# The weight and context loads of a fused attention and feed-forward kernel divided between two DMA queues by partition half

## The reference, cut to what matters

```python
def bit_quant(w):                                 # ternary weights
    scale = jnp.maximum(jnp.mean(jnp.abs(w)), 1e-8)
    return jnp.clip(jnp.round(w / scale), -1.0, 1.0)   # value in the forward pass
...
query = ctx @ Wq.T + bq            # per batch: 512 x 128
key   = ctx @ Wk.T + bk
attention = softmax(query @ key.T, axis=-1)         # 512 x 512
x = x + layernorm(x) @ attention.T
h = gelu(layernorm(x) @ bit_quant(w1).T + b1)       # w1: 2048 x 512
x = x + h @ bit_quant(w2).T + b2                    # w2: 512 x 2048
```

## Time and profile before

| | |
|---|---|
| median of 3 runs | 321.32 us (320.93 to 323.28) |
| the profiled execution | 320.93 us |
| its span in the profile | 319.1 us |
| TensorE busy | 304.6 us (95%) |
| VectorE, ScalarE, GpSimd busy | 166.8, 144.0, 117.4 us |
| DMA moved | 28.04 MB, mean 88 GB/s |
| granted TensorE clock | 1.0 throughout |

### The profile page before, as it was taken

The page is one execution under the profiler, slowest core; times in us unless marked ns, Lnnn a source line. Parts: engine busy times, 40 slices in busy tenths (PEclk is TensorE's granted clock), DMA queues, the critical chain, the costliest instruction groups (busy, mean ns, idle before and its releaser), DMA issues.

```text
span 319.1 us, 3686 instructions
## 1 busy us (share of the span) xinstructions
PE 304.6 (95%) x1397; PEld 143.7 (45%) x1397; DVE 166.8 (52%) x295; ACT 144.0 (45%) x251; POOL 117.4 (37%) x129
## 2 busy tenths in 40 slices
PE   7999979969987999999999999999999999999995
PEld 3465534434433444444444444444444444444455
DVE  2788868898689881754425630553424103342101
ACT  2287776686450652455374332456350006772000
POOL 0385369938998993000460560000470000000000
PEclk9999999999999999999999999999999999999999
DMA  8999999992100499000003947000016110000011
GB/s 198 271 209 211 213 137 219 214 278 68 31 0 0 87 175 267 0 2 0 0 0 69 174 89 199 0 0 0 2 31 130 39 66 0 0 2 0 33 62 40
DMA packets 57922, 28.04 MB, mean 88 GB/s; under 512 B 42800, under 2 KB 51760, under 8 KB 57904
## 3 DMA queue, kind: packets, MB, share of 16 engines
q1 hardware_dynamic: 57536, 27.53, 40.9%
q10 hardware_dynamic: 368, 0.27, 0.3%
HBM read 15.21 MB, written 4.19 MB: 61 GB/s over the span
## 4 chain that ended last, share of the span: by engine, by line
PE 73%; DMA 8%; SPq 8%; DVE 6%; ACT 3%; issue 2%
PE ps_e L526 31%; PE ps_t L509 29%; DMA w_raw<-in_L_ffn_w 7%; PE ps_e L494 6%; SPq L260 6%; PE ps_e L435 2%; PE ps_e L533 2%; PE ps_e L443 2%; ACT abs_out L695 1%; DVE tern L886 1%; DMA ctx_sb<-in_ctx 1%; SPq L277 1%; SPq L252 1%; DVE gT_lo L899 1%; DVE ctxT L763 1%
## 5 line engine op out<-in xcount | busy, mean ns | idle before, releaser
L509 PE MATMUL ps_t<-x2T,w1T 128*128 128x512 f16 x512 | 112.5, 379 | 0.0
L526 PE MATMUL ps_e<-w_raw,gT_hi 128*128 128x512 f16 x240 | 91.1, 380 | 3.0 <-DVE w_raw L893 3.0
L526 PE MATMUL ps_e<-w_raw,gT_lo 128*128 128x512 f16 x240 | 91.1, 380 | 0.0
L703 ACT ACTIVATE ps_t<-ps_t,b_col 128x512 f32<-128x512 f32 x64 | 42.2, 663 | 94.4 <-PE ps_t L509 94.4
L899 DVE SCALAR_TENSOR_TENSOR gT_lo<-ps_t,h_scale,gT_hi 128x512 f16<-128x512 f32 x64 | 44.9, 743 | 64.6 <-ACT gT_hi L708 64.6
L509 PEld LDWEIGHTS ps_t<-x2T,w1T 128*128 128x128 f16 x512 | 50.1, 98 | 60.6 <-issue 0.7
L905 DVE SCALAR_TENSOR_TENSOR x_sb<-ps_e,h_unscale,x_sb 128x512 f32<-128x512 f32 x15 | 11.2, 747 | 57.5 <-PE ps_e L526 57.5
L708 ACT ACTIVATE gT_hi<-ps_t,h_scale 128x512 f16<-128x512 f32 x64 | 40.3, 685 | 0.0
L526 PEld LDWEIGHTS ps_e<-w_raw,gT_hi 128*128 128x128 f16 x240 | 23.4, 98 | 33.1 <-DVE w_raw L893 4.5
L526 PEld LDWEIGHTS ps_e<-w_raw,gT_lo 128*128 128x128 f16 x240 | 23.5, 98 | 29.0 <-issue 1.7
L363 POOL TENSOR_SCALAR var_eps<-mv 128x4 f32<-128x4 f32 (+1 forms) x5 | 1.0, 196 | 81.4 <-DVE mv L835 81.4
(11 more groups left out here) (90 smaller groups left out, 276.6 us busy)
## 6 DMA issues: line engine op xcount, KB each, us to landing
w_raw<-in_L_ffn_w SPq DMA_DIRECT2D x16, 512.0 KB, 10.0
x_sb<-in_x SPq DMA_DIRECT2D x4, 1024.0 KB, 8.2
out<-x_sb SPq DMA_DIRECT2D x15, 256.0 KB, 2.5
ctx_sb<-in_ctx SPq DMA_DIRECT2D x16, 128.0 KB, 3.4
b_sb<-in_L_ffn_b SPq DMA_DIRECT2D x1, 256.0 KB, 8.6
out<-x_sb SPq DMA_DIRECT2D x2, 128.0 KB, 2.3
x2n<-in_L_xattn_Wq ACTq DMA_DIRECT2D x1, 128.0 KB, 2.9
x2n<-in_L_xattn_Wk ACTq DMA_DIRECT2D x1, 128.0 KB, 3.8
```

What stands on the lines that cost most here:

```text
L509: mm = nc.tensor.matmul(ps_t[t][:], w1T[:, k // 2, j, :, k % 2], x2T[:, b % 2, v, :, j], start=(v == 0 and j == 0), stop=(v == 1 and j == ...
L526: mm = nc.tensor.matmul(y_bank(t)[:], part[:, k, t * P:(t + 1) * P], w2T[:, k], start=(k == 0 and part is gT_hi), stop=(k == NF - 1 and pa ...
L703: nc.scalar.activation(ps_t[t][:], ps_t[t][:], ACT.Gelu, scale=1.0 / LN_SCALE, bias=b1_col[:, k:k + 1]).then_inc(gelu_done, 1)
```

## The change

Loads of the partition quarters 0 and 1 (EVEN) of both weights and of ctx 0 and 1 stay on SyncE's queue; those of quarters 2 and 3 (ODD) are issued by ScalarE, between its computations. The second half of `w2` and ctx 2 are now issued before the transposes of `x2`. ScalarE sums all eight chunks of `w2` as well, all before the first `gelus`; VectorE's `abs_sums` goes. `total(W2)` on TensorE comes before `hidden(0, 1)`. On VectorE, `turn_ctx(2)`, `abs_rows(W2)` and `quantiser_scale(W2)` come earlier.

```diff
+        EVEN, ODD = (0, 1), (2, 3)
+
+        def start_ctx(engine, b, quarters):
+            for q in quarters:
+                engine.dma_start(ctx_sb[q * R:(q + 1) * R], ctx_view[b, q]).then_inc(ctx_here, 16)
+
+        def start_w(engine, m, h, quarters):
+            n = raws[m].shape[1] // 2
+            for q in quarters:
+                engine.dma_start(raws[m][q * R:(q + 1) * R, h * n:(h + 1) * n, :],
+                                 w_views[m][q, :, h * n:(h + 1) * n, :]).then_inc(w_here[m][h], 16)
...
-            load_ctx(0)
+            start_ctx(sp, 0, EVEN)
             load_x(0)
...
-            load_ctx(1)
+            sp.wait_ge(ctxT_ready, 1)
+            start_ctx(sp, 1, EVEN)
             load_x(1)
-            load_w(0, 0)
-            load_w(0, 1)
-            load_w(1, 0)
+            start_w(sp, 0, 0, EVEN)
+            start_w(sp, 0, 1, EVEN)
+            start_w(sp, 1, 0, EVEN)
+            start_w(sp, 1, 1, EVEN)
+            sp.wait_ge(ctxT_ready, 2)
+            start_ctx(sp, 2, EVEN + ODD)
             turn_first_x2(0)
             turn_first_x2(1)
-            load_w(1, 1)
-            load_ctx(2)
...
             hidden(0, 0)
-            hidden(0, 1)
             pe.wait_ge(x2_done, 2 * NT)
             total(W2, ps_e[3])
+            hidden(0, 1)
             hidden(0, 2)
...
+            start_ctx(act, 0, ODD)
             act.dma_start(W_raw[:, 0, :], Wq).then_inc(W_here, 16)
             act.dma_start(W_raw[:, 1, :], Wk).then_inc(W_here, 16)
...
+            act.wait_ge(ctxT_ready, 1)
+            start_ctx(act, 1, ODD)
             act.wait_ge(bqk_here, 16 * 2)
             copy_qk(0)
+            start_w(act, 0, 0, ODD)
             exps(0)
+            start_w(act, 0, 1, ODD)
             copy_qk(1)
             high_turned_xn(0)
             high_turned_probs(0)
+            start_w(act, 1, 0, ODD)
+            sum_abs(0, [0])
             exps(1)
             high_turned_xn(1)
-            sum_abs(0, range(4))
+            start_w(act, 1, 1, ODD)
+            sum_abs(0, (1, 2, 3))
             high_turned_probs(1)
-            sum_abs(0, (4, 5))
-            high_x2(0, (0, 1))
-            sum_abs(0, (6, 7))
-            high_x2(0, (2, 3))
-            sum_abs(1, range(4))
+            sum_abs(0, (4, 5, 6, 7))
+            high_x2(0)
+            sum_abs(1, range(NCH))
             act.wait_ge(h_scale_done, 1)
             gelus(0, 0)
-            sum_abs(1, range(4, NCH - ABS_BY_DVE))
             gelus(0, 1)
...
             aggregate2(0, (2, 3))
-            low_x2(0, (0, 1))
             abs_rows(W1)
             residual(1, 0)
             quantiser_scale(W1)
-            low_x2(0, (2, 3))
+            low_x2(0)
+            turn_ctx(2)
             residual(1, 1)
...
             quantise(0, 3)
+            abs_rows(W2)
             low_gelus(0, (0, 1))
             quantise(0, 4)
             low_gelus(0, (2, 3))
-            abs_sums()
+            quantiser_scale(W2)
             quantise(0, 5)
             low_gelus(0, (4, 5))
-            abs_rows(W2)
+            quantise(0, 6)
             low_gelus(0, (6, 7))
-            quantise(0, 6)
-            quantiser_scale(W2)
             quantise(0, 7)
             low_gelus(0, (8, 9))
-            turn_ctx(2)
             quantise(1, 0)
```

More of the change, by code:

```diff
@@ L175, in xattn_ffn @@
         zeros_done, minus_half_done, ones_done = sem("zeros_done"), sem("minus_half_done"), sem("ones_done")
-        xn0_read, abs_by_dve = sem("xn0_read"), sem("abs_by_dve")
+        xn0_read = sem("xn0_read")
         ctxT_ready, b1_col_done, b1_abs_done = sem("ctxT_ready"), sem("b1_col_done"), sem("b1_abs_done")
@@ L193, in n_hidden @@
             return 3 + GROUPS * b + g
-        ABS_BY_DVE = 2
         def xn_bank(b, j):
@@ L247, in _ @@
         def _(sp):
-            def load_ctx(b):
-                if b:
-                    sp.wait_ge(ctxT_ready, b)
-                for q in range(Q):
-                    sp.dma_start(ctx_sb[q * R:(q + 1) * R], ctx_view[b, q]).then_inc(ctx_here, 16)
             def load_x(b):
                 sp.dma_start(x_sb[:, b], x_tiles[b]).then_inc(x_here[b], 16)
-            def load_w(m, h):
-                n = raws[m].shape[1] // 2
-                for q in range(Q):
-                    sp.dma_start(raws[m][q * R:(q + 1) * R, h * n:(h + 1) * n, :],
-                                 w_views[m][q, :, h * n:(h + 1) * n, :]).then_inc(w_here[m][h], 16)
             def turn(dst, stage, v, here):
@@ L314, in _ @@
             load_x(3)
-            load_ctx(3)
+            sp.wait_ge(ctxT_ready, 3)
+            start_ctx(sp, 3, EVEN + ODD)
             turn_x2(1)
@@ L835, in aggregate2 @@
                     nc.vector.bn_aggr(mv2[:, t], stats2[:, t]).then_inc(mv2_done, 1)
-            def abs_sums():
-                flat = w2_raw[:].rearrange("p a b -> p (a b)")
-                dve.wait_ge(w_here[1][1], 16 * Q)
-                for c in range(NCH - ABS_BY_DVE, NCH):
-                    nc.vector.tensor_reduce(abs_sum[:, 1, c:c + 1], flat[:, c * CH:(c + 1) * CH], AX.X, ALU.add,
-                                            apply_absolute_value=True).then_inc(abs_by_dve, 1)
             def abs_rows(m):
-                dve.wait_ge(abs_done, NCH if m == W1 else 2 * NCH - ABS_BY_DVE)
-                if m == W2:
-                    dve.wait_ge(abs_by_dve, ABS_BY_DVE)
+                dve.wait_ge(abs_done, NCH * m)
                 nc.vector.tensor_reduce(abs_row[:, m:m + 1], abs_sum[:, m - 1], AX.X, ALU.add).then_inc(abs_row_done, 1)
```

## The result

The changed kernel takes 330.47 us (median of 4 runs, 329.69 to 332.56) beside 321.12 us of the kernel before on the same chip: ratio 1.029, 95% interval 1.023 to 1.035. The forecast was 317.9 us, the range 316.0 to 327.0. The sign is wrong and the time lies above the range. The span of the profiled execution is 328.8 us against 319.1, +9.7.

The account below looks back on a forecast made before the run. TensorE, busy 95% of the span, was taken as the bound, so only its gaps could be won: -2.3 - 0.5 - 0.4 = -3.2 us gave 317.7, and half of the median's 0.4 on top 317.9 us; range 316.0 to 327.0.

Parts of the forecast that it names:

- The start, +0.4 us: At project(0): Wk behind two more ScalarE issues, start at 8.2 instead of 7.78 us; +0.4, bounds 0 and +0.8.
- ScalarE's issues, 1.5 us in bounds of 0 to 3: In ScalarE's queue: the fourth quarter of w1, issued behind exps(0), may block 0 to 3 us; 1.5 taken.
- The slack there is 0.97 us: On ScalarE before the second copy_qk(1) at 19.40: 0.97 us of slack to take up a blocked issue.
- Rival 4: ScalarE's issues block over 3 us or are slower; each us beyond moves hidden(0, 1) by one: 319 to 321, chance 0.15.
- The load rate, the disputed cost: Weight loads: even and odd quarters flow beside each other, 300 GB/s for w1 and 350 for w2, from 210 and 214.
- `w2` landed by 45: Sign to look for in the weight loads: w2 landed by 45 us instead of 63.64, with no wait of ScalarE.
- Nothing in the rows shows HBM or the DMA engines full: Argument for the higher weight load rates: no row shows HBM or DMA engines full at 210 GB/s.
- rival 3: Weight loads run at a rate of 240 to 280 GB/s: 319 to 324 us, chance 0.12.
- rival 2: Halves don't flow together, 210 to 225 GB/s; late ctx 2 blocks VectorE at turn_ctx(2): 326 to 330 us, chance 0.21.
- Where the gain remains: From hidden(0, 2) on: -2.3 there, -0.5 from turn_ctx(2) done early, -0.4 in output(0, 0).
- 2.6 us missing in `output(0, 0)`: Sign to look for in output(0, 0): of 3.0 us of gaps only 0.4 goes, about 2.6 us still missing.
- the sum: Whole kernel: -2.3 - 0.5 - 0.4 = -3.2 us against the profiled execution, the start inside hidden(0, 1)'s +0.5.

Follow-up runs that it names:

- e5: a with x 0 held back until ctx 0, Wq and Wk have landed, and x 1 until ctx 1 has: 323.31 us, ratio 1.008.
- e3: b with only the odd quarters of ctx 0 and 1 issued by ScalarE, weights, sums and order as before: 327.37 us, ratio 1.019.
- e11: e2 with the x2 order of b and the odd quarters of w1's second half issued behind high_turned_probs(0): 329.9 us, ratio 1.023.
- the loads alone: A separate kernel of loads only, in eleven stages, computing nothing, run once: w1 211 GB/s on one queue, 275 divided; w2 218 and 330.
- e2: a with ctx 0 and 1 wholly back on SyncE's queue, so only the weights are divided: median 324.01 us, ratio 0.999.
- e10: e2 with the order of b for high_x2, low_x2 and the sums: median 322.85 us, ratio 1.001.
- e7: b with only the two odd quarters of w2's second half issued by ScalarE, behind high_x2(0, (2, 3)): 326.02 us, ratio 1.018.
- e14: e10 with odd weight quarters issued by GpSimd: two behind x 0, two behind normalise_probs(0), four behind layernorm(1): 325.51 us, ratio 1.011.
- e8: e2 with ScalarE's later weight issues moved behind exps(1), high_turned_xn(1) and high_turned_probs(1): 327.44 us, ratio 1.017.
- e4: a with every load on SyncE's queue, in the changed order: 330.34 us, ratio 1.027.
- a: The changed kernel, against the kernel before: 330.47 us, ratio 1.029.
- e9: a with 21 warm-up products on TensorE instead of 10: 333.36 us, ratio 1.037.
- b: The kernel before the change: 321.12 us on the chip where the changed kernel was measured.

## Why the prediction was wrong

**The step that failed** is "The start, +0.4 us", with its bounds of 0 and +0.8 and "TensorE has next to no gap from there to 42.7, so it passes on". The start cost 7.3 us up to `turn_xn(0)`. I had moved Wk by two issue times and kept its 3.8 us to landing, a time measured when the whole of ctx 0 stood ahead of x 0 on the other queue and little shared with Wk. With only half the issues ahead of it, x 0 goes out at 1.70 instead of 2.76, before Wk at 2.30, and Wk and ctx share with it: 8.0 us (e5 takes the sharing away and gets the start back; e3 makes the late start alone). The ctx 1 quarters I costed at nothing; issued late behind the copy that waits for Wk, they landed 9.7 us after issue, behind nothing in their queue but beside x 1 and `w1`. And I had no term for the clock: 1.6 us in `project(0)`.

**ScalarE's issues, 1.5 us in bounds of 0 to 3.** The cause was right and the size was not: the issues took 2.79 and 5.24 us, and I had let only the first of them block. "The slack there is 0.97 us" was right for the kernel before. With the slower products behind the gaps, these two and what hangs on them moved the attention part by another 6.1 us (13.4 less 7.3). Rival 4 named the mechanism and priced it at 319 to 321, because it counted it at `hidden(0, 1)` alone and not on TensorE's own path. The reason I gave for a block, a full queue, no run shows (see e11).

**The load rate, the disputed cost.** That the halves flow beside each other was right: 275 and 330 GB/s alone, against 300 and 350 taken. In the kernel it was 217 between 15 and 28 us and 225 to 266 between 18 and 42, beside x and ctx, and the sign "`w2` landed by 45" is missing: ScalarE issued the last quarter only at 41.43, and it landed at 56.9 (63.64 before). "Nothing in the rows shows HBM or the DMA engines full" passed over the DMA share of 1.21 beside the 210 in the earlier trace rows; the loads alone show that this share doesn't tell, with 1.21 at 211 GB/s and 1.20 at 275. The rate in the kernel is that of rival 3, and below the 260 at which I let rival 2 decide; yet rival 2's path did not occur, although its 326 to 330 is close to the result: VectorE never stands before `turn_ctx(2)` (0.23 us in e2, where TensorE is on time), and the x2T wait is 0.84. Its premise, that the halves don't flow together, is refuted by the loads alone.

**Where the gain remains.** This part held, shifted by the loss. The gap before `total(W1)` is gone; what it earned is used up in waits for x2T (0.84), for `total(W2)` (0.5) and for `low_gelus` before `hidden(0, 1)` (1.02); no wait before `project(2)`; 2.6 us missing in `output(0, 0)`, as written. With the 13.4 us taken off, `hidden(0, 1)` starts 0.5 later than before and `hidden(0, 2)` 2.4 earlier, against 0.5 and 2.3 in the sum. A part of that agreement is luck: the table load came at 69.74, 56.3 without the 13.4, where I had taken 56.4 for a half-blocked ScalarE, but the 0.8 us above the unblocked 55.6 came from late x2n tiles and not from a block. From `turn_probs(1)` to the end 3.7 us were regained against 3.2 in the sum. Not foreseen was the collision of `low_x2(0)` with GpSimd's x2n tiles, 1.47 us on the way to the transposes (2.99 instead of 1.52).

So the sum fails at its start, not at its end: -3.2 for the second part stands against +13.4 for the first, for which I had written +0.4 and some of 1.5. The last sentence of the prediction, that it is wrong if landings move the attention part, had the case but gave it no chance of its own. Open stay the clock's share by itself, and whether any placing of the issues gives a version below the kernel before: of the seventeen kernels measured against it none is faster beyond its interval; e2 and e10 are level with it by the ratio (0.999 and 1.001) and 0.7 and 0.5% above it by the medians, with single executions down to 318.75 us and up to 331.

## What to carry to other kernels

A second queue is also a second claimant: a small urgent load on one queue shares with a large one on the other (here Wk went from 3.8 to 8.0 us), so hold the large one back by a wait or keep the order on one queue. Give DMA issues only to an engine that has nothing to compute while they may block; a blocked issue on SyncE delays other transfers, one on ScalarE (2.8 to 8.7 us for one, 11.55 for two here) delays also every computation queued behind it. If a matrix must be complete before its use, count the slower queue's last piece, not the mean rate, and add to each new gap of TensorE the products that then run at the lower clock.

## What the runs showed of the hardware that was not expected

- The two partition halves together: 275 against 211 GB/s with runs of 512 bytes, 330 against 218 with 2 KB; two queues on the same half at a time, 221 (512 bytes).
- Four transposing DMAs on SyncE's queue took 12.30 us instead of 8.09 with plain loads on the other queue (e7).
- Eight issues of 512 KB on GpSimd's queue took 0.58 to 1.01 us each in e14, where one of ScalarE's took 8.69 us in e8 and one of SyncE's 6.13.
- After a gap the first products took 1.4 to 1.8 times as long, but not always: `project(0)` took 3.67 us behind 1.65 us of idle time in e4, 5.23 behind 1.63 in e8, 5.37 behind 1.72 in e14, 6.67 behind 2.15 in e10. What decides is not shown.
- Two x2n tiles on GpSimd take 2.99 us beside `low_x2` of VectorE (a, e2, e9) and 1.52 or 1.53 without it (b, e8, e10).
